# Who makes the one-hots of the segment sums: VectorE or ScalarE, in three passes of row gathers of a four-layer graph network

## The chip, the cores and the metric

One core of a Trainium2 chip runs the whole program in one launch. The metric is device time in microseconds (us) from start to end of an execution; the shown time of a kernel is the median of several runs. Next to it stands one execution recorded by the hardware profiler, from which every duration below is read. Engines: PE is TensorE (matrix products), PEld its weight loads, DVE is VectorE, ACT is ScalarE, POOL is GpSimd (here it issues the gathers), SP is SyncE (it issues the plain DMAs).

## The reference

6250 nodes with 256 features, 106250 edges sorted by their target node, four layers, each of the form x = x + layer(relu(layernorm(x))):

```python
x = x + L0(h, ...)   # attention with 8 heads, segment softmax over dst
x = x + L1(h, ...)   # gated unit: two segment means, by dst of rows[src] and by src of rows[dst]
x = x + L2(h, ...)   # relational: m = segment_sum(hW[edge_type, src], dst) / deg
x = x + L3(h, ...)   # attention with edge scores, batch norm
```

Layers L1 and L2 are the two "gather layers". Their core is a segment sum:

```python
msgs = xl[src]
agg = jax.ops.segment_sum(msgs, dst, num_segments=num_nodes)
```

L1 needs it twice (once by dst, once by src, on a second order of the edges), L2 once, on rows of a table with 8 rows for each node.

## The kernel before, in words

The nodes are cut into 50 tiles of 128. The edges are padded and laid into 880 slots of 128 edges, each slot belonging to one tile of targets; the padding edges all point at the same source row, and the last slots of a pass hold nothing else. A slot is summed in four steps:

1. POOL gathers the 128 source rows of the slot from HBM with one indirect DMA (`gather_ahead`, line 818). 24 buffers are in a ring (HELD = 24), so POOL may be up to 24 slots ahead of the sums; it waits on `agg_done` once for every 4 slots.
2. A one-hot matrix says which of the 128 target nodes of the tile each edge goes to: `one_hots` (line 845) compares a row of 0..127 with the local target numbers `dl`. It makes 8 slots (a GROUP) at once, 128 partitions x 1024 values. There are two such group buffers, so the one-hots of group g+1 can be made once the products of group g-1 are done, and PE needs them when it starts group g+1.
3. PE multiplies one-hot by rows (`aggregate_run`, line 876; in float32, recorded as two matmuls a slot) into a PSUM bank.
4. DVE adds the PSUM result to the tile's sums in SBUF (`accumulate_run`, line 885).

There are three passes over the 880 slots. Pass A and pass B are in the stage `l1` and follow each other without a break (slots n = 0 to 879 and 880 to 1759 of one loop); pass C is the stage `l2`. Beside them run:

- in pass A, on DVE: after every third slot a step of a sort of the edges by source (`sort_by_source`; the merge steps are lines 488 and 489, two 128x512 operations each). Its last step sets `by_source`, which pass B needs. Fourteen times ACT copies half a turned table (line 2171) for it.
- in pass B: for each of 50 tiles, 17 slots long, DVE halves the sums of pass A, PE multiplies them with the gate weights, and ACT copies the results out of PSUM (lines 2175, 2176, 2180 and 2181). In the code ACT does this in a loop of its own, by tiles.
- in pass C, ACT has no work at all.

DVE's stream is written by hand: a loop over the slots, in each the accumulation, then, where n % 8 == 2, the one-hots of the group after, then a sort step or a halving. A stage ends when all five engines have reached its end (the semaphore `stage`).

Of the kernel before, what the change touches and what calls it, by code (L numbers as in the profile page):

```python
# [83 lines left out]
def build(nc, ctx, a, out):  # L84
# [81 lines left out]
    def prev(i, p, n=2):  # L166

        return n * i + p + 1
# [673 lines left out]
    def one_hots(dve, j, s0, h, to=oh, local=dl):  # L842
        if to is oh:
            dve.wait_ge(agg_done, prev(j, h * GROUP + GROUP - 1, RING))
        nc.vector.tensor_tensor(  # L845
            to[:, h], iota_row[:, :].unsqueeze(1).to_broadcast([P, GROUP, P]),
            local[:, bass.ds(s0 + h * GROUP, GROUP)].unsqueeze(2).to_broadcast([P, GROUP, P]),
            ALU.is_equal).then_inc(oh_ready, 1)
# [1276 lines left out]
    def l1_vector(dve):  # L2125
# [21 lines left out]
        one_hots(dve, K1, 0, 0)  # L2147
        one_hots(dve, K1, 0, 1)
        c.then(v.memset(acc[:, :], 0.0))
        sorting = sort_by_source(dve, c)  # L2150
        for n in range(2 * SLOTS):
            j, b, s = K1 + n // RING, n % RING, n % SLOTS
            if b == 0:
                places = acc_places(s, RING) if n < SLOTS else slot_places(DVE, s, RING, out_at_i, KH_AT, KHW)
            accumulate_run(dve, n, SLOTS, places[b], EDGE_PLAN, acc if n < SLOTS else kh)
            after = n + GROUP
            if n % GROUP == 2 and n > GROUP and after < 2 * SLOTS:
                one_hots(dve, K1 + after // RING, after % SLOTS // RING * RING, after % RING // GROUP,
                         local=dl if after < SLOTS else out_dl)
            if n % 3 == 1 and n < SLOTS:  # L2160
                due[n] = next(sorting, None)
            if n >= SLOTS:
                halve(*divmod(n - SLOTS, EACH))
# [3 lines left out]
    def l1_scalar(act):  # L2167
        for m in range(PHASES):
            for half, d in enumerate((1 << m, KEYS // 2)):
                act.wait_ge(cols_turned, 2 * PHASES + 2 * m + half + 1)  # L2170
                nc.scalar.copy(second.upper(half, d), blocks(ps_cols(half), d)[:, :, 1]).then_inc(upper_kept, 1)
        for k in range(TILES):
            p = k % 2
            act.wait_ge(half_ps, k + 1)
            nc.scalar.copy(g_turned[p], psum[:, 0, :].rearrange("p (c f) -> p c f", f=D))
            nc.scalar.copy(marks_row[p], psum[0:6, 1, 0:P]).then_inc(half_sb, 1)
            act.wait_ge(part_ps, k + 1)
            if k >= 2:
                act.wait_ge(part_out[p], 16 * (k // 2))
            nc.scalar.copy(g_part[p][:, 0:2], psum[:, 2, :].rearrange("p (c f) -> p c f", f=D))  # L2180
            nc.scalar.copy(g_part[p][:, 2:4], psum[:, 3, :].rearrange("p (c f) -> p c f", f=D)).then_inc(part_sb, 1)

    def l1_tensor(pe):
# [65 lines left out]
        for n in range(2 * SLOTS):  # L2249
            j, b = K1 + n // RING, n % RING  # L2250
            if n % GROUP == 0:
                pe.wait_ge(oh_ready, 2 * (j - K1) + b // GROUP + 1)
# [250 lines left out]
    def l2_vector(dve):  # L2503
        c = v_own.bind(dve)
        one_hots(dve, K2, 0, 0)
        one_hots(dve, K2, 0, 1)
# [9 lines left out]
        for n in range(SLOTS):  # L2516
# [10 lines left out]
            after = n + GROUP  # L2527
            if n % GROUP == 2 and n > GROUP and after < SLOTS:
                one_hots(dve, K2 + after // RING, after // RING * RING, after % RING // GROUP)
        dve.wait_ge(acc_done, now(K2 + ITERS - 1, RING - 1, RING))  # L2530

    def l2_tensor(pe):
        for n in range(SLOTS):
            j, b = K2 + n // RING, n % RING
            if n % GROUP == 0:
                pe.wait_ge(oh_ready, 2 * (j - K1) + b // GROUP + 1)
# [4 lines left out]
    stage_of(sync=l2_sync, gpsimd=l2_gpsimd, vector=l2_vector, tensor=l2_tensor)  # L2541
# [399 lines left out]
```

## Time and profile before

| | us |
|---|---|
| median of 3 runs | 7604.67 (7602.22 to 7616.29) |
| the profiled execution | 7620.67 |
| its span, first to last instruction | 7618.7 |
| pass A: first gather to the first gather of pass B | 2005.53 to 3180.36 |
| pass B: first gather to last gather's end | 3180.36 to 4321.41 |
| pass C: first gather to last gather's end | 4962.73 to 6104.97 |

The passes take 3458 us of the span of 7618.7. The other stages are the sort, the two attention layers, the gated unit's second part, layer norms and the batch norm. Idle time of an engine that isn't the bottleneck costs nothing. So the question for each pass is which engine never waits for another one.

### The profile page before, as it was taken

Reading aid. Unit: us, or ns where it says so; the run is one execution under the profiler, and the core shown is the slowest. Engines: PE = TensorE matmul, PEld = TensorE weight load, DVE = VectorE, ACT = ScalarE, POOL = GpSimd, SP = SyncE. Lnnn points to the kernel's source line nnn. Section 1 sums busy time; section 2 is a strip of 40 time slices with the busy share of each in tenths; the row PEclk is TensorE's granted clock in tenths of the full one; section 3 lists DMA queues with packets and bytes.
Section 4 is the critical chain, followed back from the end, with each engine's and each line's share of the span. In section 5 each row is a group of like instructions: output and inputs, shape, how many; then the busy total and the mean of one; then the engine's idle time right before and its main releaser. Section 6 shows DMA issues by size and latency. Waiting matters only on the chain. (4 is left out here: it accounts for less than half of the span.)

```text
span 7618.7 us, 77992 instructions
## 1 busy us (share of the span) xinstructions
PE 6110.5 (80%) x22430; PEld 3541.0 (46%) x22430; DVE 4883.7 (64%) x10533; ACT 1507.6 (20%) x3148; POOL 4547.8 (60%) x4618
## 2 busy tenths in 40 slices
PE   8699999998368777788888799978888857777773
PEld 4366666665233333344444344433333335555552
DVE  7799988998757666544444344444444467777767
ACT  5222222222100000000000155500000033333321
POOL 1155555554477777777777511177777727777750
PEclk9799999999675655689988799955555579898886
DMA  2266666666433333544444544433333454445553
GB/s 92 71 178 176 176 175 177 176 176 159 143 101 96 99 98 98 108 132 132 133 131 129 123 166 163 158 107 101 102 101 101 99 150 132 130 134 132 133 102 102
DMA packets 429281, 989.50 MB, mean 130 GB/s; under 512 B 119363, under 2 KB 202497, under 8 KB 422214
## 3 DMA queue, kind: packets, MB, share of 16 engines
q0 software_dynamic: 242400, 709.04, 35.4%
q1 hardware_dynamic: 186470, 275.48, 11.0%
q8 instruction: 197, 3.23, 0.2%
q14 instruction: 214, 1.75, 0.1%
HBM read 851.94 MB, written 132.00 MB: 129 GB/s over the span
## 5 line engine op out<-in xcount | busy, mean ns | idle before, releaser
L876 PE MATMUL psum<-rows,oh 128*128 128x257 f32 (+1 forms) x5280 | 2440.2, 577 | 649.3 <-DMA rows<-h_tab,src_i 190.5
L876 PEld LDWEIGHTS psum<-rows,oh 128*128 128x128 f32 x5280 | 1174.9, 264 | 1866.9 <-issue 1072.4
L885 DVE TENSOR_TENSOR acc<-acc,psum 128x257 f32 (+1 forms) x1760 | 741.6, 421 | 1110.2 <-PE psum L876 986.8
L799 POOL DMA_INDIRECT rows<-qv_tab,src_i x880 | 848.4, 964 | 848.6 <-PE psum L1060 498.0
L818 POOL DMA_INDIRECT rows<-h_tab,src_i x880 | 906.6, 1030 | 291.0 <-issue 241.7
L818 POOL DMA_INDIRECT rows<-hw_tab,rel_i x880 | 874.3, 994 | 283.9 <-issue 267.9
L818 POOL DMA_INDIRECT rows<-h_tab,wts x880 | 873.1, 992 | 268.2 <-issue 252.4
L885 DVE TENSOR_TENSOR kh<-kh,psum 128x257 f32 x880 | 371.0, 422 | 636.5 <-PE psum L876 597.4
L1400 POOL DMA_INDIRECT kh<-xh_tab,src_i x576 | 577.3, 1002 | 175.6 <-issue 123.7
L1668 DVE TENSOR_TENSOR acc<-acc,psum 128x272 f32 x880 | 378.5, 430 | 242.9 <-PE psum L1486 215.6
L1009 PE MATMUL psum<-kh,oht 128*128 x1760 | 510.6, 403 | 5.6
L1400 POOL DMA_INDIRECT rows<-xh_tab,src_i x304 | 305.4, 1005 | 221.1 <-DVEq L2878 128.8
L778 PE MATMUL psum<-acc,rows 128*128 128x512 f32 (+1 forms) x1000 | 401.2, 556 | 0.5 <-ACT rows L2413 0.5
L860 DVE TENSOR_TENSOR acc<-acc,psum 128x264 f32 x880 | 363.6, 413 | 47.5 <-issue 33.9
L1060 PE MATMUL psum<-rows,oh 128*128 128x264 f32 x1184 | 345.2, 405 | 47.6 <-issue 47.6
L1009 PEld LDWEIGHTS psum<-kh,oht 128*128 128x128 f32 x1760 | 312.8, 192 | 89.4 <-issue 47.6
L1191 DVE TENSOR_TENSOR rows<-psum,rows 128x512 f32<-128x512 f32 x440 | 300.2, 682 | 76.7 <-PE psum L1009 71.4
L2323 POOL TENSOR_TENSOR rows<-rows 128x256 f32<-128x256 f32 x50 | 31.9, 638 | 506.8 <-DMA rows<-x_tab 437.7
L1238 DVE TENSOR_TENSOR rows<-rows 128x512 f32<-128x512 f32 x440 | 291.1, 682 | 0.4 <-ACT rows L1155 0.3
L756 ACT ACTIVATE rows<-rows 128x1 f32<-128x1 f32 x150 | 30.5, 204 | 1287.2 <-DVE rows L1778 1267.7
L778 PEld LDWEIGHTS psum<-acc,rows 128*128 128x128 f32 x1000 | 186.4, 190 | 206.4 <-issue 202.8
L845 DVE TENSOR_TENSOR oh<-iota_row,dl 128x1024 f32<-128x1024 f32 x220 | 268.1, 1220 | 6.1 <-ACTq L2878 3.8
(468 smaller groups left out, 9297.2 us busy)
## 6 DMA issues: line engine op xcount, KB each, us to landing
wts<-node_rows SPq DMA_DIRECT2D x220, 256.0 KB
hw_tab<-acc SPq DMA_DIRECT2D x50, 1024.0 KB, 4.1
rows<-part_tab SPq DMA_DIRECT2D x50, 512.0 KB, 5.4
rows<-qv_tab,src_i POOLq DMA_INDIRECT x880, 3.6
rows<-h_tab,src_i POOLq DMA_INDIRECT x880, 2.8
rows<-h_tab,wts POOLq DMA_INDIRECT x880, 2.8
rows<-hw_tab,rel_i POOLq DMA_INDIRECT x880, 2.8
qv_tab<-rows SPq DMA_DIRECT2D x50, 260.0 KB, 2.0
```

The source lines that it names most:

```text
L778: mm = nc.tensor.matmul(to, ht[p][:, k * P:(k + 1) * P], w[:, k * width + at:k * width + at + size], start=k == 0, stop=k == 1)
L799: nc.gpsimd.indirect_dma_start(rows[:, b, 0:width], None, table, bass.IndirectOffsetOnAxis(index, 0)).then_inc(ring[b], 16)
L818: nc.gpsimd.indirect_dma_start(to, None, table, bass.IndirectOffsetOnAxis(index, 0)).then_inc(row_landed(m)[0], 16)
L860: nc.vector.tensor_tensor(to, to, psum[:, banks[b % len(banks)], 0:width], ALU.add).then_inc(acc_done, 1)
L876: mm = nc.tensor.matmul(slot_bank(n, plan), oh[:, n % RING // GROUP, n % GROUP], row, start=True, stop=True)
L885: nc.vector.tensor_tensor(to, to, slot_bank(n, plan), ALU.add).then_inc(acc_done, 1)
L1009: mm = nc.tensor.matmul(ps_pair(q)[:, b * D:(b + 1) * D], oht[:, h, 2 * q + b], at_place(kh, places[2 * q + b], D), start=True, stop=True)
L1060: nc.tensor.matmul(psum[:, banks[b % len(banks)], 0:ACCW], hot[(nth(j, h) - 1) % 3][:, s], rows[:, b, vat:vat + ACCW], start=True, stop=Tr ...
L1191: nc.vector.tensor_tensor(pair, ps_pair(q).rearrange("p (s f) -> p s f", s=2), pair, ALU.mult).then_inc(pair_used, 1)
L1238: nc.vector.tensor_tensor(val, val, pair[:, :, :, DH:].to_broadcast([P, 2, HEADS, DH]), ALU.mult).then_inc(msg_ready, 1)
L1400: nc.gpsimd.indirect_dma_start(held(n)[:, 0:ACCW], None, xh_tab, bass.IndirectOffsetOnAxis(src_i[:, n:n + 1], 0)).then_inc(half_landed(n / ...
L1668: nc.vector.tensor_tensor(to, to, psum[:, banks[n % len(banks)], 0:SUMW], ALU.add).then_inc(acc_done, 1)
```

## The change

ACT makes the one-hots in place of DVE, in all three passes. It takes nine instructions for a group of 8 slots: for each slot Square(local - iota), which is 0 where they agree and at least 1 where they don't, then, after a wait for its own eighth Square, one Relu(1 - square) over the whole group in place. DVE's instructions of line 845 and its waits for `agg_done` ahead of them go. ACT's stream in `l1` becomes a loop over the slots in which the one-hots and the copies of the sort and of the gates have fixed places; `l2` gets an ACT stream.

```diff
-    def one_hots(dve, j, s0, h, to=oh, local=dl):
-        if to is oh:
-            dve.wait_ge(agg_done, prev(j, h * GROUP + GROUP - 1, RING))
-        nc.vector.tensor_tensor(
-            to[:, h], iota_row[:, :].unsqueeze(1).to_broadcast([P, GROUP, P]),
-            local[:, bass.ds(s0 + h * GROUP, GROUP)].unsqueeze(2).to_broadcast([P, GROUP, P]),
-            ALU.is_equal).then_inc(oh_ready, 1)
+    squares_ready = sem("squares_ready")
+
+    def one_hots(act, g, s0, local):
+
+        of = oh[:, g % 2]
+        act.wait_ge(agg_done, RING + SLOTS + GROUP * (g - 1))
+        for s in range(GROUP):
+            sq = nc.scalar.activation(of[:, s], iota_row[:, :], ACT.Square, scale=-1.0, bias=local[:, s0 + s:s0 + s + 1])
+        sq.then_inc(squares_ready, 1)
+        act.wait_ge(squares_ready, g + 1)
+        nc.scalar.activation(of, of, ACT.Relu, scale=-1.0, bias=1.0).then_inc(oh_ready, 1)
...
-            after = n + GROUP
-            if n % GROUP == 2 and n > GROUP and after < 2 * SLOTS:
-                one_hots(dve, K1 + after // RING, after % SLOTS // RING * RING, after % RING // GROUP,
-                         local=dl if after < SLOTS else out_dl)
...
     def l1_scalar(act):
+        def hots(g):
+            if g == GROUPS:
+                act.wait_ge(by_source, 1)
+            one_hots(act, g, g % GROUPS * GROUP, dl if g < GROUPS else out_dl)
...
+        act.wait_ge(ones_set, 1)
+        hots(0)
+        hots(1)
+        for n in range(2 * SLOTS):
+            if n % GROUP == 1 and n > GROUP and n // GROUP + 1 < 2 * GROUPS:
+                hots(n // GROUP + 1)
+            what, at = due.get(n - 1) or (None, None)
+            if what == "turn":
+                keep_upper(at[0])
+            k, phase = divmod(n - SLOTS, EACH)
+            if n >= SLOTS and k < TILES:
+                if phase == 6:
+                    keep_turned(k)
+                if phase == 15:
+                    keep_part(k)
...
+    def l2_scalar(act):
+        for g in range(GROUPS):
+            one_hots(act, 2 * GROUPS + g, g * GROUP, dl)
```

## Rows read from the trace of the kernel before

**Rows 1.** The page's busy time, share and instruction count of each engine.

```profile
PE 6110.5 (80%) x22430; PEld 3541.0 (46%) x22430; DVE 4883.7 (64%) x10533; ACT 1507.6 (20%) x3148; POOL 4547.8 (60%) x4618
```

**Rows 2.** Windows in passes A, B, C: PE, PEld, DVE, ACT, POOL busy, clock, DMA share, GB/s.

```profile
2600.00:2800.00 200.00, 151.08 (x338) 76.24 (x338) 128.03 (x242) 2.93 (x5) 154.59 (x150) 0.63 0.35 98
3600.00:3800.00 200.00, 161.72 (x535) 91.60 (x535) 90.52 (x212) 16.25 (x36) 153.04 (x155) 0.93 0.45 133
5200.00:5400.00 200.00, 169.91 (x311) 74.62 (x310) 85.59 (x175) 0.00 (x0) 153.06 (x155) 0.57 0.36 102
```

**Rows 3.** Groups by line and shape: count, busy us, mean ns, idle before and its releasers.

```profile
L818 POOL DMA_INDIRECT rows<-h_tab,src_i x880 | 906.6, 1030 | 291.0 <-issue 241.7 <-PE psum L876 26.2 <-DVE rows L2145 23.1
L818 POOL DMA_INDIRECT rows<-hw_tab,rel_i x880 | 874.3, 994 | 283.9 <-issue 267.9 <-ACTq L2878 15.9
L818 POOL DMA_INDIRECT rows<-h_tab,wts x880 | 873.1, 992 | 268.2 <-issue 252.4 <-PE psum L876 15.8
L845 DVE TENSOR_TENSOR oh<-iota_row,dl 128x1024 f32<-128x1024 f32 x220 | 268.1, 1220 | 6.1 <-ACTq L2878 3.8 <-issue 2.3
```

**Rows 4.** Lines 876 and 818 in pass C: duration min/median/max in ns, first and last start.

```profile
L876 PE MATMUL psum<-rows,oh x1234: 379/634/796, 5100.2 to 5899.4; 128*128 128x256 f32 x177
...
L818 POOL DMA_INDIRECT rows<-hw_tab,rel_i x880: 942/949/2004, 4962.7 to 6104.0; - x176
```

**Rows 5.** Timeline of passes C and B (start, us, instruction, idle before): one-hots and gathers.

```profile
5306.30 0.95 POOL L818 DMA_INDIRECT rows<-hw_tab,rel_i  x1 [0.31 <-issue]
5306.72 1.22 DVE L845 TENSOR_TENSOR oh<-iota_row,dl 128x1024 f32<-128x1024 f32 x1
5307.55 1.21 POOL L818 DMA_INDIRECT rows<-hw_tab,rel_i  x1 [0.30 <-issue]
...
4308.09 1.22 DVE L845 TENSOR_TENSOR oh<-iota_row,wts 128x1024 f32<-128x1024 f32 x1
4308.15 1.98 POOL L818 DMA_INDIRECT rows<-h_tab,wts  x1 [0.30 <-issue]
```

**Rows 6.** Timeline of pass A: a merge step of the sort and the gather beside it.

```profile
2608.20 0.68 DVE L488 TENSOR_TENSOR kh<-kh 128x512 f32<-128x512 f32 x1
2608.80 0.68 DVE L489 TENSOR_TENSOR kh<-kh 128x512 f32<-128x512 f32 x1
2608.94 1.38 POOL L818 DMA_INDIRECT rows<-h_tab,src_i  x1 [0.30 <-issue]
```

**Rows 7.** Timeline of the first attention: an ACT instruction from SBUF to SBUF beside a gather.

```profile
1097.61 1.15 ACT L1115 ACTIVATE wts<-wts,small 128x1024 bf16<-128x1024 bf16 x1 [2.50 <-DMA wts<-breaks_back]
1097.89 0.95 POOL L799 DMA_INDIRECT rows<-qv_tab,src_i  x1 [2.94 <-PE psum L1060]
```

**Rows 8.** ACT's instructions of the kinds that come in, and a table load of the first stage.

```profile
L333 ACT ACTIVATE rows<-rows,oh x21: 492/496/499, 19.6 to 199.5; 128x256 bf16<-128x256 f32 x21
L1115 ACT ACTIVATE wts<-wts,small 128x1024 bf16<-128x1024 bf16 x110 | 126.3, 1148 | 319.7 <-DMA wts<-breaks_back 319.7
L2813 ACT ACTIVATE rows<-acc 128x256 f32<-128x256 f32 x48 | 19.8, 417 | 54.7 <-DVE acc L2743 54.7
L338 ACT ACT_TABLE_LOAD  x1: 1283/1283/1283, 22.2 to 22.2; - x1
```

**Rows 9.** One of ACT's three copies of 512 values a tile in pass B.

```profile
L2175 ACT COPY rows<-psum 128x512 f32<-128x512 f32 x50 | 29.3, 586 | 639.1 <-PE psum L2200 639.1
```

**Rows 10.** Timeline of pass C at its end: PE's two matmuls of one slot.

```profile
6118.35 1.19 PE L876 MATMUL psum<-rows,oh 128*128 128x256 f32 x2 [0.50 <-DMA rows<-hw_tab,rel_i]
```

**Rows 11.** Windows with line 818's busy time: before and in the tail of pass C.

```profile
6040.00:6060.00 20.00, 15.12 (x17) 0.50 0.34 101
6080.00:6100.00 20.00, 15.12 (x17) 0.50 0.97 77
```

**Rows 12.** The sort's last memsets in pass A; DVE's first work of pass C.

```profile
L2066 DVE MEMSET kh<- x5: 2200/2200/2200, 3077.8 to 3095.0; 128x2570 f32 x5
...
4962.49 2.36 DVE L845 TENSOR_TENSOR oh<-iota_row,dl 128x1024 f32<-128x1024 f32 x2 [3.79 <-ACTq L2878]
```

More of the change, by code:

```diff
@@ L2146, in l1_vector @@
         c.step(v.memset(marks6, 1.0))
-        one_hots(dve, K1, 0, 0)
-        one_hots(dve, K1, 0, 1)
         c.then(v.memset(acc[:, :], 0.0))
@@ L2167, in l1_scalar, with keep_upper, keep_turned @@
     def l1_scalar(act):
[L2168 to L2172, printed above, removed]
+        def hots(g):
+            if g == GROUPS:
+                act.wait_ge(by_source, 1)
+            one_hots(act, g, g % GROUPS * GROUP, dl if g < GROUPS else out_dl)
+        def keep_upper(k):
+            m, half = divmod(k, 2)
+            act.wait_ge(cols_turned, 2 * PHASES + k + 1)
+            d = KEYS // 2 if half else 1 << m
+            nc.scalar.copy(second.upper(half, d), blocks(ps_cols(half), d)[:, :, 1]).then_inc(upper_kept, 1)
+        def keep_turned(k):
             p = k % 2
@@ L2176, in l1_scalar, with keep_part @@
             nc.scalar.copy(marks_row[p], psum[0:6, 1, 0:P]).then_inc(half_sb, 1)
+        def keep_part(k):
+            p = k % 2
             act.wait_ge(part_ps, k + 1)
@@ L2251, in l1_tensor @@
             if n % GROUP == 0:
-                pe.wait_ge(oh_ready, 2 * (j - K1) + b // GROUP + 1)
+                pe.wait_ge(oh_ready, n // GROUP + 1)
             pe.wait_ge(*row_landed(n))
@@ L2504, in l2_vector @@
         c = v_own.bind(dve)
-        one_hots(dve, K2, 0, 0)
-        one_hots(dve, K2, 0, 1)
         c.then(nc.vector.memset(acc[:, :], 0.0))
@@ L2526, in l2_vector @@
                 fold_scores(1)
-            after = n + GROUP
-            if n % GROUP == 2 and n > GROUP and after < SLOTS:
-                one_hots(dve, K2 + after // RING, after // RING * RING, after % RING // GROUP)
         dve.wait_ge(acc_done, now(K2 + ITERS - 1, RING - 1, RING))
+    def l2_scalar(act):
+        for g in range(GROUPS):
+            one_hots(act, 2 * GROUPS + g, g * GROUP, dl)
     def l2_tensor(pe):
         for n in range(SLOTS):
-            j, b = K2 + n // RING, n % RING
             if n % GROUP == 0:
-                pe.wait_ge(oh_ready, 2 * (j - K1) + b // GROUP + 1)
+                pe.wait_ge(oh_ready, 2 * GROUPS + n // GROUP + 1)
             m = 2 * SLOTS + n
@@ L2539, in l2_tensor @@
             aggregate_run(pe, n, 3 * SLOTS, l2_rows[:, m % HELD, 0:D], REL_PLAN)
-    stage_of(sync=l2_sync, gpsimd=l2_gpsimd, vector=l2_vector, tensor=l2_tensor)
+    stage_of(sync=l2_sync, gpsimd=l2_gpsimd, vector=l2_vector, scalar=l2_scalar, tensor=l2_tensor)
     place[0] = common_end
```

## The prediction, made before the changed kernel was run

> **What bounds the kernel now.** I began with the page's busy times [rows 1]. They name PE (80%) as the busiest engine, but that is a mean over stages, and the change touches only three of them. So I cut windows out of the passes A, B and C [rows 2]. In each 200 us POOL records about 153 us of work on 150 to 155 gathers, while PE, DVE and ACT leave more room (PE at most 170 us, DVE 128, ACT 16) and the DMA engines are busy for 35 to 45%. 153 us of 200 looks like an idle quarter. The groups of line 818 say what that quarter is [rows 3]: in pass C all but 16 us of POOL's idle time is "issue", and 267.9 us / 880 is 0.30 us, the same 0.30 us ahead of every gather in the timeline [rows 5]. That is the price of issuing, not a wait. The "PE psum L876" share of passes A and B is the same 0.30 us under another name: without the 23 us ahead of the first gather, pass A has 267.9 us of idle time and pass B 268.2, again 0.30 us for each gather. POOL never waits for PE, so it sets the pace of all three passes: start to start 0.949 us [rows 4] + 0.30 us = 1.252 us for a slot, 880 x 1.252 = 1102 us for a pass. The passes measure 1175, 1141 and 1142 us. The question is what lengthens gathers.
>
> The timeline answers it [rows 5]. A gather lasts 0.95 us, except where it starts while a one-hot of line 845 is running on DVE. The gather at 5307.55 takes 1.21 us, the one at 4308.15 takes 1.98 us. In both the end lies 0.82 us behind the end of the DVE instruction: 5306.72 + 1.22 + 0.82 = 5308.76 = 5307.55 + 1.21, and 4308.09 + 1.22 + 0.82 = 4310.13 = 4308.15 + 1.98. The gather at 5306.30, already under way when the one-hot starts, isn't lengthened. So a gather needs something during its last 0.82 us that a running one-hot withholds, and DVE doesn't pay for it (1.22 us each time). The accumulations of line 885, with one operand in PSUM, don't do this: nearly every gather of pass C lies beside one, and the median is still 949 ns [rows 4]. A merge step of the sort does it too [rows 6]: 1.38 us, 0.43 more.
>
> The Trainium skill describes this ("SBUF — State Buffer", section "SBUF: two separate sides"): DVE and GpSimd share a port pair under an exclusive lock, which a DVE instruction with two SBUF inputs takes, and GpSimd writes the descriptors of its DMAs. But it limits that case to a GpSimd instruction that reads SBUF, and says the loser fully blocks. The trace agrees with the lock and adds who loses here, the gather and not DVE. The same section says that ACT has ports of its own, the trace's own evidence for which comes below.
>
> **The change, part by part.**
>
> *DVE's 330 one-hots go.* What they cost POOL, for each pass, is the excess over 880 x 0.949 = 835.1 us [rows 3, 4]. Pass C: 874.3 - 835.1 = 39.2 us. Pass B: 873.1 - 835.1 = 38.0 us. Pass A: 906.6 - 835.1 = 71.5 us, but there the sort has its share. Pairing each one-hot with the gather that starts under it gives 100 lengthened gathers in pass C, 69 in B and 72 in A, together 39.3, 37.6 and 37.7 us. In pass A some of them lie under a one-hot and a merge step both. About 36 carry a merge step as well, and one alone costs 0.27 us on the mean of 101 cases, so that the one-hots' own part is between 31 us and 37.7 us. I take 34 us. From passes B and C the last groups must be taken off: in the last 28 slots or so every edge is padding and reads the same row, the DMA engines go from 34% to 97% busy [rows 11], PE waits for landings, and POOL's pace doesn't matter. One lengthened gather lies there in B (1.03 us) and two in C (1.25 us). In pass A this backlog is taken up by pass B, because the ring holds 24 slots. Sum: 34 + 37.6 - 1.0 + 39.3 - 1.2 = 108.7 us.
>
> The 402 us of DVE time that go (330 x 1.22) are worth nothing more. DVE has 72 us free in 200 even in pass A [rows 2].
>
> *ACT's nine instructions for a group.* No row shows them in this shape. A Square of 256 values with a bias from SBUF takes 496 ns (line 333) [rows 8], 1024 values with such a bias take 1148 ns (line 1115) [rows 8], so 0.85 ns for a value and 496 - 128 x 0.85 = 387 ns for a Square of 128. Without such a bias 256 values take 417 ns, so 308 ns for 128 is the lower end. Eight Squares: 2.5 to 3.1 us; the Relu over 1024 values 1.04 to 1.15 us; one wait for its own semaphore, 0.1 to 0.3 us. That is 3.6 to 4.6 us; I take 4.3. What hides it: two group buffers. ACT may begin group g+1 when PE has ended group g-1, and PE wants it when it has ended group g, 8 x 1.252 = 10.0 us later. Cover left: 5.7 us. Were it gone, PE would wait first, then, once the 24 slots of the ring were used up (30 us), POOL.
>
> *Tables.* The first stage runs Identity, Square, Sqrt, Relu and Copy in turn, tile after tile, and after the one load on behalf of Sqrt (line 338) [rows 8] there is no other, so all five are in the set that Sqrt brings. Sqrt is the last such function ahead of both `l1` and `l2`, so I cost table loads at nothing. If Square or Relu needed another set, two loads of 1.28 us a group would make 6.9 us, still under 10.0. By the Trainium skill ("ScalarE: Activation LUTs", "What ACT_TABLE_LOAD costs") a switch with its drain is about 2.66 us: two would make an estimated 9.6 us, nearly the whole window. The rows speak against any switch.
>
> *ACT's stream in `l1`.* In pass B it also makes three copies of 0.59 us [rows 9] and a small one for each tile of 17 slots. These now stand behind one-hots. At worst, the first copy is ready just as a group's one-hots start and comes 4.3 us late, where PE wants it 3 slots (3.8 us) later. That happens for about one tile in eight, costs PE up to 1 us, and the ring hides it. The place of each copy in the loop is behind the slot in which PE makes it, so the wait for it is never earlier than the wait for `agg_done` that it precedes. `by_source` comes at 3095 + 2.2 us [rows 12], about gather 818 of 880; ACT waits for it at slot 873, so it costs nothing. In pass A the 14 copies are wanted 12 slots after they are asked for: nothing.
>
> *Beginnings.* DVE's clearing of the sums starts 2.4 us earlier, since the two first one-hots are gone [rows 12]. ACT has the first group after some 4.3 us, where DVE had it after 1.2, so PE may begin up to 3 us later. POOL, with 30 us of ring ahead of it, doesn't see that: 0, at most 2 us either way.
>
> *Who is next?* PE. At its low level of clock (granted 0.5, that is 1.2 GHz) a slot's two matmuls take 1.19 us [rows 10], under 1.252. At the higher level it takes less. So POOL stays the bound.
>
> **The sum.** Against the profiled execution: 7620.67 - 108.7 = 7512 us. That execution lies 0.2% above the median of the runs; the gain is the same count of gathers, so the median becomes 7604.67 - 108.7 = 7496 us, 1.4% less.
>
> **The rivals.**
>
> *Pass A gives its share back.* Sort steps remain, and which gather they lengthen depends on where they fall; with the one-hots gone they all shift. Only one merge step in some has a gather in the bad place now. If the steps took over all that the one-hots give up, pass A would gain nothing: 108.7 - 34 = 75 us, 7530 us. For it: merge steps and one-hots work on gathers in the same way [rows 6]. Against it: a merge step is tied to an accumulation as before, and most already meet a gather.
>
> *PE sets the pace at the low clock.* The median record of one of the two matmuls in pass C is 634 ns [rows 4], and 2 x 634 = 1.268 us is over 1.252. Then passes A and C would end at 1116 us and the gain would be about 85 us: 7520 us. Against it: the pair together takes 1.19 us [rows 10].
>
> *ACT's instructions lengthen gathers as DVE's do; slower.* ACT now reads and writes SBUF for 4.3 us of every 10. If its Relu cost a gather what a one-hot did (0.35 us) and the eight Squares met two or three more gathers at 0.27 us, a group would cost 1.0 us in place of 0.35: 330 x 0.65 = 215 us more, 7820 us. It decides from 0.35 us a group. Against it: an ACT instruction of 1.15 us, SBUF to SBUF with a bias from SBUF, has a gather start under it that takes 0.95 us [rows 7]; by the timing of rows 5 it would have taken 1.69.
>
> *Nothing changes.* The gathers could be lengthened by something that comes with the group and not by the one-hot itself, such as the end of a group in the ring. Then 7600 to 7610 us. Against it: merge steps do the same away from group ends [rows 6], and the 0.82 us is constant.
>
> **How the numbers follow.** Gain of 95 to 120 us: chance 0.70. Pass A giving back some or all: 0.12. PE at the low clock: 0.06. Nothing: 0.06. Slower by ACT's traffic or by an ACT stream that comes late: 0.04. More than 120 us, if the sort also meets fewer gathers: 0.02. The range takes in pass A's two ends and both middle rivals: 7482 to 7540 us. Less than 0.2% (15 us, about what a measurement of this kernel can tell from no change) has 0.05, slower 0.04, faster 0.91.
>
> **What would show it.** POOL's busy time for line 818 falls to some 873, 836 and 836 us, with medians still at 949 ns; pass B and C shrink to about 1103 us, A to about 1141. Gathers beside ACT's Squares and Relus stay at 0.95 us. ACT's busy time rises by some 1400 us, no table load comes in, and PE's wait for ACT in the passes is a few us. I am wrong if gathers over 1 us remain in pass C, if POOL starts to wait for PE, or if "ACT oh" is the releaser of long idle times of PE.

## The result, and the profile after

The kernel after takes 7479.85 us, median of 4 runs (7476.45 to 7483.17). The kernel before takes 7605.98 us, median of 4 runs on the same chip. The ratio is 0.9832, 95% interval 0.9815 to 0.9849: 126 us less, 1.7%. The prediction said 7496 us, so 109 us less, and 7482 to 7540. The direction and the cause were right; the gain is 17 us larger than forecast and the time lies 2 us under the low end. The interval puts the gain between 115 and 141 us, so these 2 us alone would say little; what was wrong shows in the passes.

| | before, us | after, us | difference |
|---|---|---|---|
| profiled execution, its span | 7620.67, 7618.7 | 7477.01, 7474.9 | -143.8 (span) |
| start to pass A's first gather | 2005.5 | 2002.7 | -2.8 |
| pass A, first gather to pass B's first | 1174.8 | 1126.0 | -48.8 |
| pass B, first gather to last | 1140.1 | 1099.2 | -40.9 |
| pass B's last gather to pass C's first | 642.2 | 640.6 | -1.6 |
| pass C, first gather to last | 1141.3 | 1098.9 | -42.4 |
| pass C's last gather to the edge attention's first | 129.7 | 132.9 | +3.2 |
| edge attention's gathers, and the rest | 1385.0 | 1374.6 | -10.4 |

The two profiled executions lie differently to their medians (before 14.7 us above, after 2.8 below), which is why the spans differ by more than the medians. Part of it can be seen: a gather that nothing disturbs lasts 949 ns in the one execution [rows 4] and 946 in the other, in code that the change doesn't touch as well. In a pass of 880 gathers that is 2.6 us. Without it the passes give 46.2, 38.3 and 39.8 us. The 10.4 us of the last row lie in gathers as well, of code that is the same in both kernels (882.7 us of POOL's time before, 872.3 after). In seven further executions of changed kernels, on chips that are as fast, that row is between 1369 and 1380 us, so it tells nothing of the change.

First the page's busy times of the kernel after (compare [rows 1]), then its groups by line and shape for the gathers and for ACT's new instructions (columns as in [rows 3]):

```profile
PE 6038.2 (81%) x22430; PEld 3500.6 (47%) x22430; DVE 4540.3 (61%) x10203; ACT 2658.2 (36%) x6118; POOL 4403.1 (59%) x4618
```

```profile
L818 POOL DMA_INDIRECT rows<-h_tab,src_i x880 | 857.9, 975 | 290.8 <-issue 248.2 <-DVE rows L2149 23.1 <-PE psum L880 19.5
L818 POOL DMA_INDIRECT rows<-h_tab,wts x880 | 832.4, 946 | 268.1 <-issue 246.2 <-PE psum L880 21.9
L818 POOL DMA_INDIRECT rows<-hw_tab,rel_i x880 | 832.1, 946 | 283.7 <-issue 267.8 <-SPq L2900 16.0
...
L849 ACT ACTIVATE oh<-iota_row,dl 128x128 f32<-128x128 f32 x1760 | 538.0, 388 | 1338.3 <-PE psum L880 1330.0 <-SPq L2900 6.2 <-DVE rows L2149 2.0
L852 ACT ACTIVATE oh<-oh 128x1024 f32<-128x1024 f32 x330 | 348.7, 1057 | 10.5
L849 ACT ACTIVATE oh<-iota_row,wts 128x128 f32<-128x128 f32 x880 | 269.0, 389 | 324.1 <-PE psum L880 323.9
```

Set beside [rows 3], POOL's idle time is what it was, gather for gather (291.0, 268.2, 283.9 us before); only the busy column moved: 906.6 to 857.9, 873.1 to 832.4, 874.3 to 832.1. So nothing new is waited for, and the gain in the passes is gathers that are no longer lengthened. The windows of passes A, B and C (columns as in [rows 2]) say the same of the other engines:

```profile
2600.00:2800.00 200.00, 157.44 (x365) 80.41 (x366) 110.27 (x229) 73.47 (x186) 152.18 (x158) 0.66 0.37 103
3600.00:3800.00 200.00, 165.56 (x553) 94.82 (x551) 72.84 (x202) 86.27 (x218) 151.21 (x160) 0.92 0.47 138
5100.00:5300.00 200.00, 171.42 (x321) 75.90 (x320) 67.40 (x160) 70.05 (x180) 151.25 (x161) 0.59 0.37 105
```

POOL issues 158 to 161 gathers in 200 us where it issued 150 to 155; ACT now works 70 to 86 us of 200 and PE is at most 171. The timeline of pass C shows one group being made on ACT, with the gathers beside it:

```profile
5201.02 0.95 POOL L818 DMA_INDIRECT rows<-hw_tab,rel_i  x1 [0.30 <-issue]
...
5201.44 2.44 ACT L849 ACTIVATE oh<-iota_row,dl 128x128 f32<-128x128 f32 x8 [6.50 <-PE psum L880]
5202.27 0.95 POOL L818 DMA_INDIRECT rows<-hw_tab,rel_i  x1 [0.30 <-issue]
...
5203.52 0.95 POOL L818 DMA_INDIRECT rows<-hw_tab,rel_i  x1 [0.30 <-issue]
...
5203.91 1.06 ACT L852 ACTIVATE oh<-oh 128x1024 f32<-128x1024 f32 x1
5204.77 0.95 POOL L818 DMA_INDIRECT rows<-hw_tab,rel_i  x1 [0.30 <-issue]
```

The gather at 5202.27 starts under the Squares, the one at 5204.77 under the Relu, and both last 0.95 us. The chain takes 3.53 us a group (5201.44 to 5204.97), and ahead of it ACT waited 6.5 us for PE. The line of starts and durations for pass C's gathers (compare the second line of [rows 4], where the longest takes 2004 ns) leaves no exception:

```profile
L818 POOL DMA_INDIRECT rows<-hw_tab,rel_i x880: 942/946/958, 4868.5 to 5967.4; - x176
```

### The profile page after: what moved, and what is told of

Same layout as the page of the kernel before. It is cut to its first block and busy times, and to the rows that moved or that the text cites. A ratio compares the mean times of both kernels' runs of the same rounds, so it can differ in the third digit from the quotient of the medians.

```text
span 7474.9 us, 80633 instructions
## 1 busy us (share of the span) xinstructions
PE 6038.2 (81%) x22430; PEld 3500.6 (47%) x22430; DVE 4540.3 (61%) x10203; ACT 2658.2 (36%) x6118; POOL 4403.1 (59%) x4618
## 3 DMA queue, kind: packets, MB, share of 16 engines
q0 software_dynamic: 242400, 709.04, 36.2%
## 5 line engine op out<-in xcount | busy, mean ns | idle before, releaser
L880 PE MATMUL psum<-rows,oh 128*128 128x257 f32 (+1 forms) x5280 | 2384.8, 564 | 621.8 <-DMA rows<-h_tab,src_i 210.9
L880 PEld LDWEIGHTS psum<-rows,oh 128*128 128x128 f32 x5280 | 1148.5, 258 | 1809.6 <-issue 993.8
L818 POOL DMA_INDIRECT rows<-h_tab,src_i x880 | 857.9, 975 | 290.8 <-issue 248.2
L849 ACT ACTIVATE oh<-iota_row,dl 128x128 f32<-128x128 f32 x1760 | 538.0, 388 | 1338.3 <-PE psum L880 1330.0
L818 POOL DMA_INDIRECT rows<-hw_tab,rel_i x880 | 832.1, 946 | 283.7 <-issue 267.8
L818 POOL DMA_INDIRECT rows<-h_tab,wts x880 | 832.4, 946 | 268.1 <-issue 246.2
L849 ACT ACTIVATE oh<-iota_row,wts 128x128 f32<-128x128 f32 x880 | 269.0, 389 | 324.1 <-PE psum L880 323.9
L852 ACT ACTIVATE oh<-oh 128x1024 f32<-128x1024 f32 x330 | 348.7, 1057 | 10.5
```

Source lines behind the costliest of these rows:

```text
L818: nc.gpsimd.indirect_dma_start(to, None, table, bass.IndirectOffsetOnAxis(index, 0)).then_inc(row_landed(m)[0], 16)
L849: sq = nc.scalar.activation(of[:, s], iota_row[:, :], ACT.Square, scale=-1.0, bias=local[:, s0 + s:s0 + s + 1])
L852: nc.scalar.activation(of, of, ACT.Relu, scale=-1.0, bias=1.0).then_inc(oh_ready, 1)
L880: mm = nc.tensor.matmul(slot_bank(n, plan), oh[:, n % RING // GROUP, n % GROUP], row, start=True, stop=True)
```

## The experiments

The theory: a DVE instruction that reads two operands from SBUF keeps a gather from ending until 0.82 us behind its own end, and DVE's one-hots were such instructions. The rivals: the gain comes from something else that went with them (DVE's waits, its load, the place in the loop). Beside it stands the question of what made the surplus of 17 us. Kernels called "after with ..." are the kernel after with the edit shown. Times are medians; a ratio is to the kernel before on the same chip.

### One pass back on DVE at a time

The edit adds DVE's former instruction as a helper and uses it in one pass alone, where the kernel before had it; ACT's stream leaves that pass out.

```diff
+    def dve_one_hots(dve, g, s0, local, times=1):
+        dve.wait_ge(agg_done, RING + SLOTS + GROUP * (g - 1))
+        for _ in range(times):
+            ins = nc.vector.tensor_tensor(
+                oh[:, g % 2], iota_row[:, :].unsqueeze(1).to_broadcast([P, GROUP, P]),
+                local[:, bass.ds(s0, GROUP)].unsqueeze(2).to_broadcast([P, GROUP, P]), ALU.is_equal)
+        ins.then_inc(oh_ready, 1)
...
+            g = n // GROUP + 1
+            if n % GROUP == 2 and n > GROUP and g < GROUPS:
+                dve_one_hots(dve, 2 * GROUPS + g, g * GROUP, dl)
...
-    def l2_scalar(act):
-        for g in range(GROUPS):
-            one_hots(act, 2 * GROUPS + g, g * GROUP, dl)
```

After with pass A's one-hots on DVE. 

> The changed kernel with the one-hots of pass A alone back on VectorE. The predicted size for pass A was 34 us: 7480 + 34 = 7514 us. The comparison of the two traces says 46 us (pass A 48.8 us shorter, 2.6 of them because every gather was 3 ns shorter in that execution): 7526 us. If the second is right, the gathers lengthened by merge steps of the sort also rise again, from 73 to about 104.

After with pass B's. 

> The changed kernel with the one-hots of pass B alone back on VectorE. By the lengthened gathers 37 to 38 us more: 7518 us. If the parts don't add up, since one pass changes the clock or the state in which the next begins, the sum of the three runs of this kind will differ from 126 us.

After with pass C's (the diff above). 

> The changed kernel with the one-hots of pass C alone back on VectorE. 38 to 40 us more, some 100 gathers lengthened, each ending 0.82 us behind the end of a one-hot: 7519 us.

Measured: 7525.91, 7516.12 and 7513.76 us (ratios 0.9901, 0.9895, 0.9888, each within 0.0017), so 46, 36 and 34 us over the kernel after, 116 of the 126 us in all. That kernel ran on another chip, though; by the ratios, each to the kernel before on its own chip, the three are 52, 48 and 43 us, so from the medians no share is known to better than some 10 us. POOL's busy time is the finer measure. The groups of line 818, one from each kernel, its own pass:

```profile
L818 POOL DMA_INDIRECT rows<-h_tab,src_i x880 | 906.6, 1030 | 291.0 <-issue 246.0 <-DVE rows L2161 23.1 <-PE psum L892 21.9
```

```profile
L818 POOL DMA_INDIRECT rows<-h_tab,wts x880 | 871.9, 991 | 268.3 <-issue 248.2 <-PE psum L892 20.1
```

```profile
L818 POOL DMA_INDIRECT rows<-hw_tab,rel_i x880 | 874.4, 994 | 283.7 <-issue 267.7 <-ACTq L2913 15.9
```

Each pass is back at its value in [rows 3] (906.6, 873.1, 874.3), and the passes that stay on ACT remain at 861 to 865, 832 to 835 and 834.5 us. The share of each pass is its own: a pass that goes back leaves the gathers of the other two short. Pass A's busy time over 880 undisturbed gathers is 71.5 us with DVE's one-hots, in the kernel before and in this one, and 25.4 to 29.8 us in the six executions with ACT's. So pass A's share is 42 to 46 us, not 34; the kernel after's own profiled execution is the one at the upper end.

### What in the instruction holds the gather

After with pass C's one-hots on DVE, one operand in PSUM: the row 0..127 is copied once into a free bank, and the products use six banks in place of eight.

```diff
-    EDGE_PLAN, REL_PLAN = ((4, 5, 6, 7), 2, KHW), (range(8), 4, D)
+    EDGE_PLAN, REL_PLAN = ((4, 5, 6, 7), 2, KHW), (range(6), 4, D)
...
+        c.then(nc.vector.tensor_copy(psum[:, 7, 0:P], iota_row[:, :]))
...
+                oh[:, g % 2], psum[:, 7, 0:P].unsqueeze(1).to_broadcast([P, GROUP, P]),
```

> Pass C's one-hots on VectorE again, but the row 0..127 is read from PSUM, so that the instruction has one operand in SBUF in place of two; 12 result places of 256 in six PSUM banks in place of 16 in eight, to make room. If the second SBUF operand is what holds the gathers up: no lengthened gathers in pass C, 7480 us. If it is VectorE's being busy at that point of a group: 39 us more, 7519 us.

It landed on a chip of the kind told of further down, on which nothing could be read from the time (8342.49 us, ratio 1.0017); the gathers' busy time in pass C was 832.0 us. The same kernel once more:

> The same kernel as c_psum, on a chip on which POOL's pace sets the passes, if it comes to one. Pass C's one-hots on VectorE with the row 0..127 in PSUM. Second SBUF operand as the cause: POOL's busy time in pass C 832 to 835 us, pass C as short as in the changed kernel (1099 us from first to last gather). VectorE's being busy as the cause: 874 us and 1141 us.

7472.26 us, ratio 0.9825 (0.981 to 0.984). The group of its one-hots and the timeline of pass C:

```profile
L849 DVE TENSOR_TENSOR oh<-psum,dl 128x1024 f32<-128x1024 f32 x110 | 133.8, 1217 | 0.0
```

```profile
5206.93 1.22 DVE L849 TENSOR_TENSOR oh<-psum,dl 128x1024 f32<-128x1024 f32 x1
5207.61 0.94 POOL L818 DMA_INDIRECT rows<-hw_tab,rel_i  x1 [0.30 <-issue]
```

The instruction is as long as before (1.22 us), runs on the same engine at the same place in the loop, and a gather starts under it and lasts 0.94 us; by [rows 5] it would have ended 0.82 us behind DVE, at 5208.97, so would have lasted 1.36. Line 818 takes 832.0 us in this pass. In the whole pass 101 gathers start under such an instruction early enough to be held, and no gather of the pass lasts over 0.962 us; in the kernel before 183 of 189 are held under line 845 with the table `dl`. Beside the place of the operand only the number of PSUM banks differs (six in place of eight), and passes A and B, which were held, use four. So the second SBUF operand is the cause, and neither the wait nor DVE's load is. The Trainium skill ("SBUF — State Buffer", section "SBUF: two separate sides") names this lock for a DVE instruction with two SBUF inputs, "only against a GpSimd op that reads SBUF". The traces agree with two SBUF inputs, and that limit is no objection: each gather reads its 128 row numbers from SBUF (`src_i`, `rel_i` and, in pass B, a part of `wts`). The same section says that whichever starts first has the ports for the whole instruction; here DVE isn't held by a gather that is under way (the one-hot at 5306.72 in [rows 5] takes its 1.22 us). Its figure of DVE's end + about 115 ns is for a DMA issued by GpSimd beside a tensor_copy of DVE. Here the gather ends 0.81 to 0.84 us behind DVE's end in the cases shown, so it is the last 0.82 us of its 0.95, or all but its first 0.13 us, that follow the release. Whether it is the reading of the row numbers or the writing of the descriptors that waits, no run tells.

After with pass C's one-hots made twice on DVE, first into an unused buffer:

```diff
+        for k in range(times):
+            if times == 2 and k == 0:
+                v_own.wait()
+            ins = nc.vector.tensor_tensor(
+                (oht if k < times - 1 else oh)[:, g % 2], iota_row[:, :].unsqueeze(1).to_broadcast([P, GROUP, P]),
+                local[:, bass.ds(s0, GROUP)].unsqueeze(2).to_broadcast([P, GROUP, P]), ALU.is_equal)
```

> Pass C's one-hots on VectorE, each made twice in a row (the first time into an idle buffer), so that VectorE is at it for about 2.4 us without a gap. If a gather that starts meanwhile ends 0.82 us behind the end of the work: each of some 100 gathers grows by 1.2 us more, in all 39 + 130 = 165 to 175 us more than the changed kernel, 7650 us. If each instruction costs a fixed price: 78 us more, 7558 us.

On the chip of that kind: 8343.58 us, ratio 1.0015, line 818 in pass C at 890.4 us. Once more:

> The same kernel as c_twice, on a chip on which POOL sets the pace, if it comes to one. Each one-hot of pass C made twice in a row. By the rule that a gather that starts meanwhile ends 0.82 us behind the end of VectorE's work: POOL's busy time in pass C 835 + 39 + 130 = 1000 to 1010 us. By a fixed price for each instruction: 913 us.

7515.97 us, ratio 0.9883 (0.9868 to 0.9898), line 818 in pass C at 883.5 us. Neither expectation was met: twice the DVE time lengthens pass C's gathers by 51 us (883.5 - 832.5) where once does by 42. By the ends, 102 gathers are held by the first instruction of a pair, with 42.5 us, as by a single one, and only 8 by the second, with 8.2 us. The timeline shows why:

```profile
5201.54 1.22 DVE L851 TENSOR_TENSOR oht<-iota_row,dl 128x1024 f32<-128x1024 f32 x1
5202.35 1.22 POOL L818 DMA_INDIRECT rows<-hw_tab,rel_i  x1 [0.30 <-issue]
...
5202.68 1.22 DVE L851 TENSOR_TENSOR oh<-iota_row,dl 128x1024 f32<-128x1024 f32 x1
5203.81 0.41 DVE L905 TENSOR_TENSOR acc<-acc,psum 128x256 f32 x1
5203.88 0.95 POOL L818 DMA_INDIRECT rows<-hw_tab,rel_i  x1 [0.30 <-issue]
```

The gather at 5202.35 ends at 5203.57, 0.81 us behind the end of the first instruction (5202.76), although the second is running by then. It slips in between the two, and the next one starts when the second is all but over. The hold is for one instruction, and the excess of a gather is bounded by the length of one instruction, not by that of a block of them. The merge steps show it too: 36 gathers of pass A in the kernel before end 0.82 us behind line 488, and line 489 is running at that moment in all 36.

### Where pass A's other 12 us come from

I paired each gather that takes over 0.03 us more than 0.95 us, by durations to 0.01 us, with the DVE instruction whose end lies 0.82 us ahead of the gather's end (within 0.06). (Where an undisturbed gather lasts 946 ns this leaves out a few that are lengthened by 0.03 us; with each execution's own median the kernel after has 78 gathers and 20.3 us in the last column.) In pass A, as count and excess in us:

| kernel, pass A | all lengthened | by one-hots | by merge steps, lines 488 and 489 |
|---|---|---|---|
| before | 213, 71.7 | 88, 38.1 | 104, 27.9 |
| after | 107, 25.1 | 0 | 73, 19.8 |
| after, A on DVE | 208, 71.5 | 83, 37.7 | 100, 27.0 |
| after, B on DVE | 105, 30.1 | 0 | 78, 23.9 |
| after, C on DVE | 101, 27.6 | 0 | 74, 21.7 |
| after, C with a PSUM operand | 106, 26.8 | 0 | 76, 21.4 |
| after, C made twice | 112, 29.6 | 0 | 85, 24.6 |
| after, reduction in A | 132, 36.2 | 0 | 104, 30.6 |
| after, order in A | 118, 29.4 | 0 | 85, 22.1 |

The nine executions come from chips on which the kernel before takes 7600 us. The one-hots' own part is 38 us, and with them gone the merge steps, which nobody touched, lengthen fewer gathers: 73 to 85 in the six executions with ACT's one-hots in A and nothing in their place, 100 to 104 with 1.2 us more of DVE work a group. (On chips of the kind told of below, where the passes have another rhythm, it is 101 before and 98 after, so this second effect isn't seen there.) To see if it is DVE's time itself that does it, a reduction of the same length was put in the one-hots' place:

```diff
+            if n % GROUP == 2 and n > GROUP and n + GROUP < SLOTS:
+                nc.vector.tensor_reduce(idle_sums[:, :], iota_row[:, :].unsqueeze(1).to_broadcast([P, GROUP, P]), axis=AX.X,
+                                        op=ALU.add)
```

> The changed kernel, and in pass A, at the places in VectorE's stream where the one-hots stood, a sum over 1024 values of SBUF that nobody reads: some 1.2 us of VectorE's time with one SBUF operand. Theory 1, the one-hots cost pass A more than their own gathers because the time that they take on VectorE moves the sort's steps to a bad place: merge steps lengthen about 100 gathers again (100 with the one-hots on VectorE, 73 without), 8 to 12 us more than the changed kernel. Theory 2, the lengthened gathers themselves moved the sort's steps against POOL: no change, 73. If any VectorE instruction on SBUF lengthens gathers: 34 us or more.

7484.72 us, ratio 0.9842 (0.9828 to 0.9855), and line 818 in pass A, with the reduction's group:

```profile
L818 POOL DMA_INDIRECT rows<-h_tab,src_i x880 | 869.0, 987 | 290.8 <-issue 252.2 <-DVE rows L2150 23.1 <-PE psum L881 15.5
...
L2160 DVE TENSOR_REDUCE idle_sums<-iota_row 128x8 f32<-128x1024 f32 x108 | 130.8, 1211 | 0.0
```

869.0 us against 857.9 in the kernel after and 859.7 to 864.9 in four other executions with the same pass A (864.9 where an undisturbed gather lasts 949 ns, so 862.3 at 946). The timeline shows that the reduction holds no gather itself, and neither do the others in the pass: 82 gathers start under one early enough to be held, and none is.

```profile
2598.67 1.21 DVE L2160 TENSOR_REDUCE idle_sums<-iota_row 128x8 f32<-128x1024 f32 x1
2599.35 0.95 POOL L818 DMA_INDIRECT rows<-h_tab,src_i  x1 [0.30 <-issue]
...
2602.63 0.75 DVE L2031 TENSOR_SCALAR kh<-kh,small 128x1024 f32<-128x1024 f32 x1
2603.11 1.08 POOL L818 DMA_INDIRECT rows<-h_tab,src_i  x1 [0.30 <-issue]
```

So the 6 to 11 us more come from the merge steps, which are back at 104 lengthened gathers: with 1.2 us of DVE time ahead of them more gathers start under them. That is a second effect of the change in pass A, of 8.1 us in the two profiled executions (27.9 - 19.8; 3 to 8 over the six), beside the one-hots' own 38. Its size in the total time (4.9 us) is within what two medians differ by; the counts and POOL's busy time carry it, for the reduction from one execution. The last line shows a further kind of instruction that holds a gather, with one large operand in SBUF: it ends at 2603.38 and the gather at 2604.19, 0.81 us later.

Could the steps be moved on purpose? The sort's step ahead of the accumulation:

```diff
-            accumulate_run(dve, n, SLOTS, places[b], EDGE_PLAN, acc if n < SLOTS else kh)
...
+            accumulate_run(dve, n, SLOTS, places[b], EDGE_PLAN, acc if n < SLOTS else kh)
```

> The changed kernel with each sort step of pass A ahead of the accumulation of its slot in place of behind it: the same work, 0.4 us earlier in VectorE's stream, waiting for nothing that it didn't wait for. If it is the place of the sort's steps against POOL's gathers that decides what they cost, pass A's 25 us of lengthening (73 gathers by merge steps) change by 10 us or more, either way. If each merge step has a fixed chance to meet a gather: within 3 us of 25.

7478.51 us, ratio 0.9836 (0.9822 to 0.9849), line 818 in pass A at 863.1 us, 85 gathers under merge steps. Pass A's lengthening is 29.4 us, within the 25.1 to 30.1 of the executions with this pass A, so it didn't move by 10 us or more as the first theory had it.

### How much cover ACT has

After with more work for ACT in pass C: 16 further Squares for a group into an unused buffer (some 8.3 us a group), or these and two Relus of 2048 values (12 us).

```diff
+            act.wait_ge(extra, done)
+            for s in range(2 * GROUP):
+                sq = nc.scalar.activation(oht[:, s // GROUP, s % GROUP], iota_row[:, :], ACT.Square, scale=-1.0,
+                                          bias=dl[:, s:s + 1])
+            sq.then_inc(extra, 1)
+            done += 1
+            for _ in range(2):
+                act.wait_ge(extra, done)
+                nc.scalar.activation(oht_flat, oht_flat, ACT.Relu, scale=-1.0, bias=1.0).then_inc(extra, 1)
+                done += 1
```

> The changed kernel, and in pass C ScalarE makes 16 more Squares after each group, into an idle buffer: 3.5 + 4.8 = 8.3 us of its time for a group of 10.0 us. ScalarE is hidden: no change, 7480 us, and no gather longer, though ScalarE now works for most of the time. If ScalarE's SBUF traffic costs gathers anything: tens of us.

> As the run with 16 more Squares, and two Relus over 2048 values beside: 3.5 + 4.8 + 4.1 = 12.4 us of ScalarE's time for a group. Now ScalarE must set the pace of pass C: 110 x (12.4 - 10.0) = 264 us more, 7744 us, and POOL waits. If the cover were larger than worked out: less.

> The kernel after, with so much more work for ScalarE in pass C that a group takes it some 12 us in place of 3.5, on a chip where the kernel before takes some 7600 us. Theory (the cover of ScalarE's one-hots is the group's own length, 8 slots x 1.25 = 10.0 us): PE waits for ScalarE, then POOL for PE; pass C 110 x 12.0 = 1320 us in place of 1099, so some 220 us less 30 us of ring at the start: 7670 to 7705 us. Rival (nothing waits as long as the ring holds rows): 7480 us. Line 818 stays at 832 us busy.

> The same with some 8.3 us for a group, under 10.0. Theory: the cover holds, 7480 us within 10 us, line 818 in pass C at 832 us busy. Rival (a one-hot that comes late in its group already costs): 7500 us or more.

All seven runs of the two kernels fell on chips on which the kernel before takes 8330 to 8460 us, so the forecasts of time, made for 7600, can't be held against them. 12 us: 8416.54, 8421.75, 8418.69 and 8534.32 us, ratios 1.0115, 1.0097, 1.0095 and 1.0081 (each within 0.003). 8 us: 8345.15, 8354.28 and 8466.70 us, ratios 1.0027 (1.0015 to 1.004), 1.0025 (1.001 to 1.004) and 1.0002 (0.9983 to 1.0021). Two of the three are clear of 1, and on one of these chips the kernel after itself stands at 0.9996: there 8.3 us a group cost some 20 us, though they are under 10.0. That bears out the rival, that a one-hot which comes late in its group already costs, at least on these chips. What the 12 us do can be read from the timeline all the same (the last of the four, pass C):

```profile
5700.82 1.06 ACT L852 ACTIVATE oh<-oh 128x1024 f32<-128x1024 f32 x1
...
5701.79 4.77 ACT L2557 ACTIVATE oht<-iota_row,dl 128x128 f32<-128x128 f32 x16
...
5705.99 0.95 POOL L818 DMA_INDIRECT rows<-hw_tab,rel_i  x1 [2.26 <-PE psum L880]
5706.59 3.85 ACT L2563 ACTIVATE oht<-oht 128x2048 f32<-128x2048 f32 x2
...
5710.34 2.43 ACT L849 ACTIVATE oh<-iota_row,dl 128x128 f32<-128x128 f32 x8
...
5712.80 1.06 ACT L852 ACTIVATE oh<-oh 128x1024 f32<-128x1024 f32 x1
...
5713.77 4.77 ACT L2557 ACTIVATE oht<-iota_row,dl 128x128 f32<-128x128 f32 x16
5713.91 6.07 PEld L880 LDWEIGHTS psum<-rows,oh 128*128 128x128 f32 x16 [6.74 <-ACT oh L852]
```

ACT never rests, a group has a period of 11.98 us (5700.82 to 5712.80), PE waits for ACT and POOL for PE: 110 x 11.98 = 1318 us, and the pass takes 1310.0 (5422.6 to 6732.6). With 8.3 us a group it takes 1264.9, and 1256.7 in the kernel before on that chip. So at 12 us the bound is ACT. Where between 3.53 and 12 us it begins to cost, on a chip where a group takes 10.0 us, was not measured, and the prediction's cover isn't tested there beyond 3.53. ACT's load lengthens no gather: they stay at 832.2 us in pass C with ACT's group more than twice as long.

### A chip on which the change is worth nothing

The kernel after, once more, on a chip where the kernel before takes 8332 us:

> The changed kernel itself, unaltered. On a chip on which the kernel before takes some 7600 us: 7480 us, as measured. On a chip on which it takes some 8330 us and POOL stands still for other reasons for a fifth of each pass: if the gathers' own time still sets the pace between those pauses, 126 us less; if what a gather saves is taken up by the pauses, no difference (8330 us).

8330.43 us, ratio 0.9996 (0.998 to 1.0012). And the kernel before, to have its profile on such a chip:

> The kernel before, unchanged, for its profile on this chip. On a chip where it takes some 7600 us: pass C 1141 us, 100 gathers lengthened. On a chip where it takes some 8330 us, where the change was worth nothing: the gathers are lengthened all the same (line 818 at 906, 873 and 874 us busy), and the passes are as long as after the change (1285, 1290, 1245 us), the difference lying in POOL's idle time.

8454.07 us. Its gathers, and then those of passes A and B of the kernel after with ACT's 8 us in pass C, which is the kernel after in these two passes and ran on the same chip:

```profile
L818 POOL DMA_INDIRECT rows<-h_tab,src_i x880 | 903.5, 1027 | 421.7 <-issue 249.1 <-PE psum L876 95.0 <-remote 54.5
...
L818 POOL DMA_INDIRECT rows<-h_tab,wts x880 | 868.6, 987 | 415.3 <-issue 245.4 <-remote 106.3 <-PE psum L876 63.6
```

```profile
L818 POOL DMA_INDIRECT rows<-h_tab,src_i x880 | 862.0, 980 | 448.4 <-issue 241.7 <-remote 97.5 <-PE psum L880 86.0
L818 POOL DMA_INDIRECT rows<-h_tab,wts x880 | 832.2, 946 | 456.8 <-issue 242.2 <-remote 129.2 <-PE psum L880 85.4
```

The gathers are lengthened before and not after, as on the other chips: POOL's busy time falls by 77.9 us in the two passes. But the idle time ahead of them rises by 68.2 us, from 837.0 to 905.2, and 65.9 of it is "remote": an idle time whose end fits no recorded instruction of this core. From A's first gather to B's last it is 2585.1 us before and 2575.3 after. In the timeline of such a chip (the kernel after, pass C) engines come out of it at the same instant, within 0.24 us:

```profile
5646.32 2.44 ACT L849 ACTIVATE oh<-iota_row,dl 128x128 f32<-128x128 f32 x8 [7.16 <-remote]
5646.32 2.00 DVE L889 TENSOR_TENSOR acc<-acc,psum 128x256 f32 x4 [5.08 <-remote]
5646.56 0.94 POOL L818 DMA_INDIRECT rows<-hw_tab,rel_i  x1 [1.02 <-remote]
```

All three wait in the kernel for one semaphore, `agg_done`, which PE raises, so they need nothing else in common than that it rises late. And the word "remote" says little here, since the traces of these chips lack about half of the semaphore events (56350 in this one, 110443 in the kernel after's on the first chip). Of the gathers of pass C even the landing time is missing, first on that chip, then here:

```profile
rows<-hw_tab,rel_i POOLq DMA_INDIRECT x880, 2.8
```

```profile
rows<-hw_tab,rel_i POOLq DMA_INDIRECT x880
```

What can be read is that in pass C PE waits there for the one-hots, whoever makes them (after, then before: us in total, times, longest). On the fast chip this wait is 0.6 us before, and it isn't found after.

```profile
PE psum L880 <- ACT oh L852: 519.7, 61, 20.8
```

```profile
PE psum L876 <- DVE oh L845: 498.1, 54, 23.5
```

So the gathers don't set the pace on these chips, and a shorter gather only waits longer. PE waits for the one-hots, and their engine waits for PE's `agg_done`; what makes this round late stays open, and no run here tells it.

## Why the prediction was right or wrong

**What bounds the passes: right.** POOL does, before and after; its idle time is the price of issuing in both. Its busy time was forecast at 873, 836 and 836 us and came out at 857.9, 832.4 and 832.1; B and C are right once 2.6 us are allowed for, by which this execution's undisturbed gathers are shorter.

**Passes B and C: right.** Forecast 36.6 and 38.1 us less; the passes gave 40.9 and 42.4, or 38.3 and 39.8 at 949 ns a gather. Put back on DVE they cost 36.8 and 41.9 us of POOL's busy time over undisturbed gathers.

**Pass A: the step that failed.** It was put at 34 us, between 31 and 37.7, and gave 48.8 (46.2 at 949 ns; 42 to 46 over the six executions). Two statements were wrong. The first took 3.7 us off because some gathers lie under a one-hot and a merge step both. By the ends, 88 gathers end behind a one-hot, with 38.1 us, and when the one-hots went the merge steps took over none of it: their own part fell. (By the prediction's own numbers, 36 gathers at 0.27 us, the lower bound would have been 28 us, not 31.) The second was "The 402 us of DVE time that go are worth nothing more". DVE had room in every window, and that was the reason given; but in pass A its time also places the merge steps, and 104 gathers lengthened by them became 73, 8 us less. The reduction in the one-hots' place brought the 104 back. "The sort also meets fewer gathers", which is what happened, was given 0.02. The low end of the range, 7482 us, follows from no term: with A's upper bound of 37.7 us the sum is 112.4 us, 7492 us. With 38.1 + 8.1 us for A it would have been 120.9 us, 7484 us, 4 us from the measured time. Of the 17 us that were missing, pass A has 12 by the kernel after's own execution (8 by the lower end of the six), B and C have 1.7 each, and 1.3 are the two medians of the kernel before.

**ACT's group: cheaper than taken.** Forecast 3.6 to 4.6 us, taken at 4.3; it is 3.53, just under the low end. The Square of 128 values takes 388 ns, as worked out from [rows 8] (387), but the next one starts some 294 ns after it (2.44 us for eight), not 388; the sum of durations was the upper bound and should have been taken as that. By the Trainium skill ("ScalarE: Activation LUTs", "What ACT_TABLE_LOAD costs") such an instruction takes 280 + 0.833 x 128 = 387 ns and back-to-back ones overlap by 93 ns, an estimated 294; the trace agrees with both. A group of PE's products takes 10.0 us, so the miss was worth nothing. No table load came in: ACT's loads are the same, 51 and 50 at the two lines that have many of them.

**PE, and ACT's copies: right.** The longest waits of PE in the passes are for landing gathers (210.9, 167.9 and 137.2 us), as before (190.5, 163.3 and 123.5); ACT's one-hots are no large releaser in any group. On the chips told of last they are, with DVE's one-hots just as with ACT's, so the prediction's sign of being wrong is met there without the change as its cause. POOL's waits for PE in A and B, 19.5 and 21.9 us, are as small as in [rows 3]. PE kept up though its clock was at the lower level, 1.2 GHz, for most of pass C (granted 0.59 on the mean of the window).

**The tail: not shown.** 1.2 us had been taken off for pass C, because POOL's pace doesn't matter in its last slots. Up to the next gather it is 132.9 us in place of 129.7, but the nine executions lie between 126.4 and 132.9 with no order by kernel, so a term of this size can't be read.

**The rivals.** Pass A giving back its share went the other way. ACT's traffic lengthens nothing: no gather of pass C takes over 958 ns, and with ACT at 8.3 us a group their mean stays at 946 ns. PE at the low clock didn't come to be the bound (above). "Nothing changes" is what happened on other chips, but not for the reason given: the gathers were shortened there too. That the pace might be set by neither engine, depending on the chip, was in no case of the prediction.

## What to carry to other kernels

Where POOL issues gathers one after the other, look at what DVE runs at the moment at which they start: here a tensor_tensor with both operands in SBUF holds one gather until it is done, and moving one operand to PSUM was worth as much as moving the work to ACT (ratio 0.9825 with pass C done in that way, 0.9832 without). The sum of such excesses is read by pairing ends, 0.82 us apart here. Where other instructions of the same kind share the stream, freeing DVE also moves those, so a range has to be open on that side even if DVE has idle time. What a change is worth is to be read on more than one chip.

## What the runs showed of the hardware that was not expected

- The hold is for one instruction: of two 1.22 us instructions back to back the gather waits for the first alone (883.5 us in place of 874.4 for one).
- Held by: tensor_tensor with two SBUF operands (1.22 and 0.68 us), and a tensor_scalar of 1024 values in 0.75 us (4 of the 4 gathers that start under one in time, in the kernel with the reduction), which has one large operand only. So two SBUF operands are one way to hold a gather and not the only one. Not held by: tensor_tensor with one operand in PSUM (1.22 us, 101 gathers), tensor_reduce (1.21 us, 82 gathers), ACT's Square and Relu.
- The edge attention's gathers lie at 994 and 987 ns on the mean beside DVE's line 1664 (before: 1002 and 1005, where the same statement is line 1660), two SBUF operands of 128x512 in 684 ns. By the ends 150 of them are held by it, with 36 of the 40 us by which these 880 gathers exceed 946 ns each. Taking that away was not tried.
- Chips differ: the kernel before takes some 7600 us on at least two of them, 8330 to 8460 us on three, with the same durations of gathers and one-hots and more idle time of POOL between them.
